# Adjacency loops counted in one-hots, the first norm chunk by chunk, edge weights widened by ScalarE

## The reference

```python
xn = _layernorm(x, axis=-1)
x = x + _L0_gnn_ref(xn, L0_gnn_weight, edge_weight, src, dst) + _L0_mix_ref(xn[None], ...)[0]
x = x + _L0_ffn_ref(_layernorm(x, axis=-1)[None], ...)[0]
# then a graph attention (two layers), a linear attention and a second mixture of experts
```

## Time and profile before

| what | us |
|---|---|
| median of three runs | 1158.15 (1157.52 to 1159.11) |
| the profiled execution | 1156.29 |
| its span in the trace | 1154.5 |
| start of the span to the first matmul of the loops | 44.5 |
| the loops (222 one-hots in 37 iterations) | 44.5 to 132.3 |
| everything behind them | 132.3 to 1154.5 |

### The profile page before, as it was taken

How to read it: one execution, slowest core, us unless ns; L and a number is a source line. 1 busy time by engine, 2 the same in 40 slices (tenths; PEclk the granted TensorE clock), 3 DMA queues, 4 the chain that set the end, 5 groups by cost and what they waited for, 6 DMA issues and landing times.

```text
span 1154.5 us, 20380 instructions
## 1 busy us (share of the span) xinstructions
PE 1095.8 (95%) x7337; PEld 738.7 (64%) x7338; DVE 562.2 (49%) x1431; ACT 369.6 (32%) x931; POOL 116.3 (10%) x182
## 2 busy tenths in 40 slices
PE   3888999999999999999999799999999999999999
PEld 2577746457777565555455477877477878755664
DVE  7888755845446421122112444544233455587651
ACT  1011322035556312221122345544114454412530
POOL 1012380020000020111010440000000000001000
PEclk9999999999999959999999999999999999999999
DMA  4100374200000169910699850000210000010001
GB/s 131 37 1 2 91 178 186 83 19 28 28 11 1 76 230 395 401 36 14 262 396 404 306 204 28 29 9 21 73 55 28 29 28 1 1 37 0 1 0 45
DMA packets 21404, 112.72 MB, mean 98 GB/s; under 512 B 5127, under 2 KB 6904, under 8 KB 15198
## 3 DMA queue, kind: packets, MB, share of 16 engines
q1 hardware_dynamic: 15864, 100.95, 23.4%
q0 software_dynamic: 5472, 10.83, 3.6%
HBM read 102.78 MB, written 8.98 MB: 97 GB/s over the span
## 4 chain that ended last, share of the span: by engine, by line
PE 82%; DVE 7%; DMA 4%; issue 4%; ACT 2%; DVEq 1%; POOL 1%; SPq 0%; POOLq 0%; ACTq 0%
PE psum L807 10%; PE psum L625 9%; PE psum L1004 8%; PE psum L981 7%; PE psum L830 6%; PE psum L861 6%; PE psum L812 5%; PE psum L843 5%; PE psum L692 4%; PE psum L1126 3%; PE psum L1031 3%; PE psum L1104 3%; PE psum L643 3%; DMA arena<-in_moeW 3%; PE psum L764 2%
## 5 line engine op out<-in xcount | busy, mean ns | idle before, releaser
L625 PE MATMUL psum<-arena 128*125 128x512 f32 x320 | 140.0, 593 | 1.0 <-ACT arena L1198 0.7
L1228 ACT ACTIVATE arena<-arena,small 125x625 f32<-125x625 f32 x120 | 97.0, 809 | 89.9 <-DVE small L1621 89.9
L807 PE MATMUL psum<-arena 128*128 128x313 f32 (+1 forms) x384 | 111.6, 439 | 2.8 <-ACT arena L1167 1.9
L625 PEld LDWEIGHTS psum<-arena 128*125 128x125 f32 x320 | 59.2, 188 | 73.9 <-issue 70.1
L1303 ACT ACTIVATE arena<-psum,cols 128x64 f32<-128x64 f32 x224 | 47.6, 360 | 182.2 <-PE psum L990 182.2
L1004 PE MATMUL psum<-arena 128*64 128x256 f32 x896 | 100.0, 381 | 1.6 <-DMA arena<-in_moeW 1.5
L981 PE MATMUL psum<-arena 128*64 128x512 f32 x448 | 99.9, 598 | 1.1 <-DMA arena<-in_moeW 0.5
L807 PEld LDWEIGHTS psum<-arena 128*128 128x128 f32 x384 | 70.9, 192 | 32.1 <-issue 3.4
L1621 DVE CUSTOM_DVE_ANT_0 arena<-psum,cnt_adj 125x625 f32<-125x625 f32 x80 | 61.5, 806 | 57.3 <-PE psum L830 57.3
L1236 ACT ACTIVATE arena<-psum 125x500 f32<-125x500 f32 x120 | 63.7, 583 | 73.2 <-PE psum L843 73.2
L692 PE MATMUL psum<-arena 125*128 x1110 | 69.8, 221 | 17.0 <-DVE arena L1515 17.0
(11 more groups left out here) (297 smaller groups left out, 1430.5 us busy)
## 6 DMA issues: line engine op xcount, KB each, us to landing
arena<-in_moeW SPq DMA_DIRECT2D x32, 2048.0 KB, 18.3
arena<-in_att SPq DMA_DIRECT2D x36, 256.0 KB, 2.7
arena<-in_l1W SPq DMA_DIRECT2D x2, 2048.0 KB, 12.1
token_rows<-arena POOLq DMA_DIRECT2D x19, 128.0 KB, 4.9
rows<-in_rows SPq DMA_DIRECT2D x1, 2240.0 KB
expert_rows<-arena POOLq DMA_DIRECT2D x17, 128.0 KB, 4.8
arena<-in_gnnWo SPq DMA_DIRECT2D x2, 1024.0 KB, 5.9
arena<-token_rows POOLq DMA_DIRECT2D x14, 128.0 KB, 6.9
```

The lines of the kernel that those rows point to most:

```text
L625: mm = pe.matmul(bank(b, NP, D), srcT[:, k, c * NP:(c + 1) * NP], w[:, k, :], start=(k == 0), stop=(k == KC - 1))
L807: mm = pe.matmul(bank(b, P, width), aw[:, w, k, :], srcT[:, k, o:o + width], start=(k == 0), stop=(k == KC - 1))
L1228: act.activation(Sx[u % 3][h], Sx[u % 3][h], ACT.Exp, bias=small[0:NP, 80 + n:81 + n], scale=-1.0, accum_out=small[0:NP, 120 + n:121 + n]) ...
```

## The change

It has four parts.

1. **Loops.** The loop variable `n` counts one-hots over all windows, in steps of six. Window w runs from `ends[w]` to `ends[w + 1]`, numbers that are loaded to registers as they are used. Waits are on `n + s + 1`, and the tile is `n + shifts[w] + s`. So two rows of 20 numbers are loaded instead of one, and nothing is unpacked.
2. **First norm.** x comes in ten DMAs, two for each chunk, each chunk with a semaphore of its own; the graph weight is issued without a wait for x. DVE takes each chunk's moments and normalizes the one before it, ahead of the windows' numbers. ACT takes five small square roots, and its table is loaded early. PE takes turned chunks and graph products in turns.
3. **Weights.** ACT copies each weight part over the 32 nodes into `hot_dst`, in three thirds for each part (nine copies), and DVE multiplies that in place with the plain one-hot, also in nine pieces. The comparison is cut in two.
4. **Order.** The loops' numbers are loaded to registers on PE ahead of the last `hp` product, and on DVE ahead of the last three pieces. `hot_free` starts at six from the beginning of PE's program. PE also executes seven products of a constant with itself, into a PSUM bank that nobody reads (`keep_busy`).

```diff
+ENTRY = [("xnT0", 0), ("xnT0", 1), ("hp", 0), ("xnT0", 2), ("hp", 1), ("xnT0", 3), ("hp", 2), ("xnT0", 4), ("hp", 3),
+         ("hp", 4)]
-ORDER = ["xnT0", "hp", "mq", "mk", ...
+ORDER = [ENTRY, "mq", "mk", ...
+        THIRDS = [slice(i * TP // 3, (i + 1) * TP // 3) for i in range(3)]
...
         def window_ranges(engine):
-            _, values = nc.values_load_multi_w_load_instructions(bounds[0:1, 0:NW], engines=[engine], min_val=1,
-                                                                 max_val=NW * KG * 16384 + 64 * ET + KG)
-            return values
-
-        def tile_range(eng, packed):
-            return (eng.snap((packed >> 6) & 255, min_val=0, max_val=ET - 1), eng.snap(packed & 63, min_val=1, max_val=KG),
-                    eng.snap(packed >> 14, min_val=0, max_val=(NW - 1) * KG))
+            first, second = [nc.values_load_multi_w_load_instructions(
+                bounds[0:1, o:o + NW], engines=[engine], min_val=-NW * KG * GT, max_val=NW * KG * GT,
+                skip_runtime_bounds_check_because="the program clamps a window's first tile and its count")[1]
+                for o in (0, NW)]
+            return [0] + list(first), second
@@ SP
-            for p in SPLIT:
-                sp.dma_start(xres[p], ins["x"][p]).then_inc(ld_x, 16)
-            sp.wait_ge(ld_x, 32)
+            for c in range(NC):
+                for p in SPLIT:
+                    sp.dma_start(xres[p, c, :], ins["x"][p, c, :]).then_inc(ld_x[c], 16)
             sp.dma_start(ring[0], ins["gnnW"]).then_inc(ld_ring[0], 16)
@@ PE
-            rows_to_cols("xnT0", N1, lambda c: pe.wait_ge(ln_out, c + 1))
...
-            product_rows("hp", T1, 0)
-            pe.wait_ge(range_ready, 1)
-            ranges = window_ranges(mybir.EngineType.PE)
+            def keep_busy(b, n, w):
+                for _ in range(n):
+                    pe.matmul(bank(b, P, w), onesf[:], onesf[:, 0:w], start=True, stop=True)
+
+            pe.nop().then_inc(hot_free, GT)
+            keep_busy(5, 5, P)
+            for stage, c in ENTRY:
+                if stage == "xnT0":
+                    pe.wait_ge(ln_out, c + 1)
+                    turn_chunk("xnT0", N1, c)
+                    if c == 0:
+                        keep_busy(5, 2, P)
+                    continue
+                if c == 0:
+                    ring_ready(0)
+                stage_out(pe, "xnT0", c + 1)
+                product_chunk("hp", T1, ring[0], c)
+                if c == 0:
+                    pe.wait_ge(range_cols, 1)
+                    pe.matmul(bank(7, NW, WMIN), upper[0:NW, 0:NW], w_loops, start=True, stop=True).then_inc(range_cum, 1)
+                if c == 1:
+                    pe.wait_ge(range_cols, 2)
...
+                if c == 3:
+                    pe.wait_ge(range_ready, 1)
+                    ends, shifts = window_ranges(mybir.EngineType.PE)
...
             for w in range(NW):
-                first, k, before = tile_range(pe, ranges[w])
...
-                with pe.Fori(0, k) as j:
+                with pe.Fori(ends[w], ends[w + 1], GT) as n:
                     for s in range(GT):
-                        e = nc.s_assert_within(first + j * GT + s, 0, TP - 1,
+                        e = nc.s_assert_within(n + shifts[w] + s, 0, TP - 1,
-                        pe.wait_ge(hot_ready, (before + j) * GT + s + 1)
+                        pe.wait_ge(hot_ready, n + s + 1)
@@ ACT
-            deviation(0)
-            cols_out("xnT0", T1)
-            rows_out("hp", N2)
+            act.activation(small[0:1, 94:95], onesf[0:1, 0:1], ACT.Sqrt)
+            def widened(v, i):
+                t_ = THIRDS[i]
+                act.wait_ge(edge_parts, v + 1)
+                act.activation(hot_dst4[:, t_, v, :], w_part[:, v, t_].unsqueeze(2).to_broadcast(
+                    [NP, t_.stop - t_.start, DW]), ACT.Copy).then_inc(wide_parts, 1)
...
+            widened(0, 0)
+            widened(0, 1)
+            chunk_deviation(0, 0)
+            chunk_deviation(0, 1)
+            chunk_cols_out("xnT0", T1, 0)
...
+            hp_out(2)
+            chunk_cols_out("xnT0", T1, 4)
+            widened(2, 1)
+            widened(2, 2)
+            hp_out(3)
+            hp_out(4)
@@ DVE
-            for c in range(NC):
-                i_ = chunk_stats(xres, c)
-            link(i_)
-            norm_moments()
+            for c in range(NC):
+                ve.wait_ge(ld_x[c], 32)
+                chunk_moments(xres, c)
+                if c:
+                    chunk_normal(0, xres, N1, c - 1)
+            chunk_normal(0, xres, N1, NC - 1)
...
-            norm_apply(0, xres, N1)
-            ve.wait_ge(range_cum, 1)
...
+            for h, t_ in enumerate((slice(0, TP // 2), slice(TP // 2, TP))):
+                n = t_.stop - t_.start
+                ve.tensor_tensor(hot_dst4[:, t_, 3, :], low[:, t_].unsqueeze(2).to_broadcast([NP, n, DW]),
+                                 iota_dst.unsqueeze(1).to_broadcast([NP, n, DW]), ALU.is_equal).then_inc(dst_one, 1)
+                if h == 0:
+                    ve.wait_ge(range_cum, 1)
...
             for v in range(3):
-                ve.tensor_tensor(hot_dst4[:, :, v, :], hot_dst4[:, :, 3, :],
-                                 w_part[:, v, :].unsqueeze(2).to_broadcast([NP, TP, DW]), ALU.mult).then_inc(dst_parts, 1)
+                for i, t_ in enumerate(THIRDS):
+                    ve.wait_ge(wide_parts, 3 * v + i + 1)
+                    ve.tensor_tensor(hot_dst4[:, t_, v, :], hot_dst4[:, t_, v, :], hot_dst4[:, t_, 3, :],
+                                     ALU.mult).then_inc(dst_parts, 1)
+                if v == 0:
+                    ve.wait_ge(range_rows, 1)
+                    ve.tensor_copy(bounds, bank(3, 1, WMIN)).then_inc(range_ready, 1)
+                if v == 1:
+                    ve.wait_ge(range_ready, 1)
+                    ends, shifts = window_ranges(mybir.EngineType.DVE)
```

More of the change, by code:

```diff
@@ L218, in build @@
         w_end = take(NW, 8)
-        w_cols = take(NW, 3)
+        w_cols = take(NW, 4)
         w_loops = take(NW, WMIN)
@@ L285, in build @@
         ld_edges, ld_const, ld_rows = sem("ld_edges"), sem("ld_const"), sem("ld_rows")
-        ld_x = sem("ld_x")
+        ld_x = [sem(f"ld_x{c}") for c in range(NC)]
         ld_ring = [sem(f"ld_ring{i}") for i in range(2)]
@@ L667, in _ @@
-            pe.wait_ge(range_ready, 1)
-            ranges = window_ranges(mybir.EngineType.PE)
+            def keep_busy(b, n, w):
[19 more added lines that the diff above has]
+                    pe.wait_ge(range_cols, 2)
+                    stage_out(pe, "xnT0", 3)
+                    for v in range(2):
+                        mm = pe.matmul(bank(3, 1, WMIN - NW * v, NW * v), w_cols[:, 2 + v:3 + v],
+                                       ident[0:NW, 0:WMIN - NW * v], start=True, stop=True)
+                    mm.then_inc(range_rows, 1)
+                if c == 3:
+                    pe.wait_ge(range_ready, 1)
+                    ends, shifts = window_ranges(mybir.EngineType.PE)
@@ L1508, in _ @@
             for w in range(NW):
-                first, k, before = tile_range(ve, ranges[w])
-                with ve.Fori(0, k) as j:
+                with ve.Fori(ends[w], ends[w + 1], GT) as n:
                     for s in range(GT):
-                        e = nc.s_assert_within(first + j * GT + s, 0, TP - 1,
+                        e = nc.s_assert_within(n + shifts[w] + s, 0, TP - 1,
                                                skip_runtime_bounds_check_because="a window's tiles end below TP")
-                        ve.wait_ge(hot_free, (before + j) * GT + s + 1)
+                        ve.wait_ge(hot_free, n + s + 1)
```

55 lines of the change are left out of this document (29 added, 26 removed).

## The result

The changed kernel took 1149.74 us (median of 4 runs, 1148.34 to 1150.62); the kernel before took 1157.84 beside it (1156.58 to 1159.11). The ratio is 0.9937 with a 95% interval of 0.9918 to 0.9956: faster by 8.1 us. I had forecast 1137.5 and 1131.5 to 1147. The sign is right, the size and the range are wrong: 20.6 us were forecast and 8.1 came.

A forecast was written before the change was run, and what follows sets the result against it. The prediction saw the entry bound by a DVE chain and the loops by PE's sequencer. Entry 6.0 plus loops 14.6 gave 20.6 off 1156.29, so 1135.7; with 1.9 kept for the median, 1137.5 us, range 1131.5 to 1147.

The forecast's parts named there:

- The register loads: Entry: DVE's two loads, 1.62 us each, delay its last three products about 0.4; PE's take 3.2, stalling 0 to 0.5.
- DVE as the next bound: Loops: with PE's iteration at 1.88 us DVE is late next; 1.96 taken for 30 later iterations, 2.07 for window 0's seven.
- Rival 1: Loops: DVE with POOL's interference, or mutual buffer waits, holds an iteration at 2.1; loops give 7.4, time 1144.8; chance 17%.
- The sequencer's share in the loops: Loops: PE's sequencer sheds three operations and shortens two fused ones, saving 0.43 to 0.44 us per iteration, bounds 0.38 and 0.49.
- The entry otherwise: Entry: products 1.0 us apiece, window numbers at 21.0, PE stalled for them from 19 to 21, nine widening copies covered.
- Clock at its full level from 22 on: Entry onward: a sign of the forecast, TensorE's clock at its full level from 22 us on.
- Rival 4: Entry and window 0: the new idle stretch drops TensorE's clock to 1.2 GHz, costing 23 us, time 1160; chance 2%.
- The rest: Behind the loops: nothing edited, carried over unchanged; the forecast is wrong if it is not 1022 us long within 2.

The follow-up runs named there:

- before_odd: Kernel before with only its column tile one word wider, so its register load reads from 92980 instead of 92976; 1160.65 us (one run).
- loads_16: Changed kernel plus one register and-operation per window and three unused words, so register loads read from 92992 and 93072; 1145.47 us, ratio 0.9885 to the kernel before.
- no_pool: Changed kernel plus one register and-operation per window, without GpSimd's two additions per window; only loops read: 73.2 to 73.4 us, windows after the first 58.65.
- half_hot: Changed kernel plus one register and-operation per window, VectorE writing only 314 of 628 one-hot columns; only loops read: 73.2 to 73.4 us, windows after the first 58.8.
- before_loops: Kernel before with the new loops alone and two register loads per engine at the old places, entry untouched; 1147.15 us, ratio 0.9915.
- before_loops_16: As before_loops, with columns padded so both register loads read from multiples of 16 (92992, 93072); 1146.76 us, ratio 0.9883 to the kernel before.
- moved: As loads_16, with the two small products of the window numbers one entry product later on TensorE; 1140.85 us, ratio 0.9828 to the kernel before.

## Why the prediction was wrong

- **The register loads** ("DVE's two register loads, 1.62 each"; "a stall of 0 to 0.5"): the first step that failed, and the larger. The duration was read from a row of the kernel before and carried to a new place in memory. They took 4.5 to 4.9. DVE stood for 6.41 and TensorE for 4.87 us, and the product behind ran at half clock for another 1.5. before_odd shows the cause on one word, loads_16 the cure: 8.0 us at the first loop product, which then comes at 38.10 where the forecast had 38.4. The stated bounds held no room for this, because I gave that row no bound at all.
- **DVE as the next bound** ("I take 1.96 for the 30 later iterations, halfway"): wrong, this is the second step that failed. It is 62.80 / 30 = 2.09. I had counted GpSimd's interference from the kernel before, 18 slow one-hots, as 0.25 a window. Now 37 are slow, about two a window, each by 0.29 us, so 0.55 a window. That cost 4.1 us. no_pool and half_hot show that DVE is the bound, and no_pool that the additions make it so.
- **Rival 1** ("an iteration only falls to 2.1", 17%): right in its mechanism and its pace, wrong in its price. It gave the loops a gain of 7.4 and they gained 10.5 (87.9 to 77.4): window 0 fell from 2.50 to 2.09 an iteration, the others from 2.35 to 2.09. The 7.4 were reckoned as 0.2 for each of 37 iterations. With 10.5 and the forecast entry its time would have been 1141.6 and not 1144.8. That 1144.8 lies nearer to the measured time than my forecast is luck, since it has no slow loads in it.
- **The sequencer's share in the loops** ("Sum 0.43 to 0.44"): right in the mechanism and at its lower bound (0.38) in size. Fused operations took 46 and up to 80 ns. Window 0 took 14.61 / 7 = 2.09 (2.07 forecast), 0.41 less than before. With DVE relieved the others take 1.96, which is 0.39 less. For TensorE I had 1.88, counted from one iteration of 2.31 where the mean was 2.35. That its 1.96 equals the figure that I took for DVE is luck.
- **The entry otherwise**: right. Products 1.0 us, DVE's chain to 20.6 (21.0), the new stall for the window product 1.84 us, nine widening copies of 1.66 us hidden by the gaps. The x chunks were never waited for.
- **"Clock at its full level from 22 on"**: wrong in the changed kernel, whose second product runs at 0.50 from 22.3 to 25.6 and takes 5.30. Here that was hidden by the later wait for the loads, which end at 39.6 whatever the products do. Rival 4's 23 us never came near: the two half-clock stretches of the entry lengthened their products by 1.7 and 1.5 us.
- **The rest** ("not 1022 us long within 2"): 1024.1, just inside; 1.5 of the 1.9 lie in the 11th stretch, by the clock.

Check of the sum: 1149.25 less 7.6 (entry), 4.1 (loops) and 1.9 (rest) is 1135.65, my 1135.7 for the profiled execution. The 1.9 that I added to it for the median was 0.5 here (1149.74 against 1149.25).

What stays open:

- Why a load is slow from these addresses: the runs show that it is, and not why.
- Why an addition on GpSimd and a one-hot on VectorE wait for each other. No other kinds of operations were tried.
- What besides a pause makes the clock halve. Ahead of the loops, too, pauses of 2.02 and 2.04 us had half clock behind them (the kernel before and before_loops), and one of 2.07 had not (before_loops_16); each was followed by a shorter one (1.25, 0.73 and 0.74).
- Why 6.0 us between the traces of loads_16 and before_loops_16 are 1.3 between their medians, and where the 4.6 us of moved come from.
- Why window 0 takes 2.09 an iteration on TensorE where the others take 1.96. It does so in no_pool and half_hot as well.
- What the seven constant products (`keep_busy`), the chunked norm and the copies on ScalarE are worth each. No run takes one of them out; only the whole entry was compared.

## What to carry to other kernels

A duration in a trace belongs to an instruction at an address. Where a change widens or inserts a tile in a packed memory, list what moves behind it, and give every operation that reads from there a range and not a number; then look first at the start address when an unchanged instruction changes its duration. And where a change takes the pauses out of one engine, count what other engines had been doing in the pauses of its partner: the interference read off the slack kernel was half of what came (18 slow one-hots, then 37).

## What the runs showed of the hardware

- The clock of TensorE (second product of the entry): half of its level for 3.4 us behind pauses of 1.84, 1.98 and 2.41 us, full behind pauses of 1.53, 1.65, 1.72 and 2.42, in eight kernels with the same wait.
- A load of 20 registers from on-chip memory took 1.37 to 1.63 us from byte addresses 92976, 92992 and 93072 (multiples of 16), and 4.49 to 4.93 from 92980, 92984, 93060 and 93064 (not multiples of 16, two of them of 8), on VectorE and TensorE alike, alone or both at once.
- Dense two-tensor bf16 products on VectorE took 1052 to 1076 ns for 1760 elements per partition, against 5.6 us for 5280 with a broadcast operand before.
- GpSimd's first addition of a window (160 float32 per partition) took 604 ns in the median and up to 4112 beside unbroken one-hots of VectorE. Nearly each addition (37 of 40) held up one one-hot, to about 660 ns for 375, and that one ended 178 to 186 ns after the addition.
